# Graph layers: 24,000 of 100,000 edges counted once into small matrices and multiplied, the others gathered as before

## The chip, the cores and the metric

One Trainium2 chip, one of its cores. The metric is the device time of one launch in microseconds (us). TensorE (PE) multiplies, VectorE (DVE) and ScalarE (ACT) work elementwise, GpSimd (POOL) issues the indirect DMAs (gathers and scatters), SyncE (SP) issues the plain ones. SBUF has 128 partitions; PSUM has eight banks of 128 x 512 f32.

## The reference

3125 nodes with 256 features, 100,000 edges (src, dst, relation 0 to 3), all f32. Cut to what matters:

```
h   = x @ W0                                       # first layer
x   = layernorm(x + segment_sum(h[src] * norm, dst))
cnt[dst, type] += 1;  inv = 1 / max(cnt[dst, type], 1)
for l in 0..3:                                     # four relational layers
    h   = einsum('ni,rio->rno', X, weights[l])     # 4 tables of 3125 x 256
    agg = segment_sum(h[type, src] * inv, dst)
    out = agg + X @ root[l] + bias[l]
    X   = elu(layernorm(out) * gamma + beta) + X
result = layernorm(x + X)
```

The sources are drawn evenly over the nodes; the targets are the square of a uniform number, so low nodes have many edges.

## The kernel before, in words

Nodes are cut in 25 **windows** (NW) of 128 by target. The kernel has a set-up and five passes over the edges (q = 0 for the first layer, 1 to 4 for the relational ones).

**Set-up.** Edges lie as 125 x 800 in SBUF. DVE counts the edges of each window (L783), works out how many tiles of 128 edges each window needs, orders the windows by size, and gives every edge its rank in its window: a loop over the 25 windows (L839 to L851) of a hit row (L834), a running sum (L845) and a predicated copy (L851). Then the edges are sorted into tiles (L893 on, PE L554 to L567): in 50 iterations of 16 edge columns, 10 columns are placed by one-hot matmuls (L563, tile_hot against a 806-column row in two halves) and 6 by scatters of POOL (L408). L566 counts edges per node and relation. DVE decodes the placed edges (L926 to L943). There are NT = 806 tiles, a bound that is known before the run.

**A pass** does for each tile t, in this order of dependence:
- POOL gathers 128 rows of 256 f32 from the table of h in DRAM (L425) into one of RING = 20 slots. Gather n waits until the product of tile n - 20 is done (L424).
- A 128 x 128 **edge matrix** (one-hot of target times weight) is written into a ring of BODY = 32: in pass 0 by ACT (L681 Square, L690 Relu), later by DVE (L951), HALF = 16 tiles ahead.
- PE multiplies edge matrix and gathered rows into one of NPS = 6 banks (L533).
- DVE adds the bank to the accumulator of the tile's window (L976). The window's number comes from a list that is loaded into registers eight at a time (L961). In pass 0 DVE also finds each edge's weight first (L968).

Each engine's order is written out by hand. A window is complete after tile done_at[j] = (j + 1) * NT // 25. Its **window work** follows at fixed tiles after that: DVE norm and activation (L1031 to L1066, at +0 to +11), ACT Sqrt, Exp and copies (L607, L618, L622 to L637, each waiting its turn in one queue), PE transpose (L482, +15), four products of 512 columns with the next layer's weights (L490, +19 to +22) and the root product (L500, L503, +26, +27). SP writes the window's new rows of h to DRAM (L365). Pass q + 1 starts its gathers when the last window's rows are written (L421).

PE's matmul in f32 appears in the trace as two records, so a product of one tile is "x2".

Of the kernel before, what the change touches and what calls it, by code (L numbers as in the profile page):

```python
# [19 lines left out]
def build_program(nc, x, src, dst, etype, w0, weights, roots, biases, gammas, betas, out,  # L20
                  h0_table, h_tables, inv_dram, x1_dram, placed_dram):
    f32, f16, i32 = mybir.dt.float32, mybir.dt.float16, mybir.dt.int32
    ALU = mybir.AluOpType
# [14 lines left out]
    NT = (E + NW * (P - 1)) // P  # L38
    HALF = 16
    BODY = 2 * HALF  # L40
    RING = HALF + 4
    WINS = 8


    done_at = [(j + 1) * NT // NW for j in range(NW)]
    NPS = 6
# [5 lines left out]
    HB = NT // 2  # L52
    assert HB * 2 == NT and HB <= 512 and EC % SU == 0
# [6 lines left out]
    LOW = 1 << LOWBITS  # L60

    ctx = ExitStack()
    with ctx:
# [3 lines left out]
        def sem(name):  # L67
# [7 lines left out]
        iota16 = sb("iota16", [P, NT], f16)  # L75
        zeros16 = sb("zeros16", [P, 512], f16)
# [12 lines left out]
        X1 = arena[:, 0:NW * D]  # L89
# [3 lines left out]
        msg = sb("msg", [P, HALF, D])  # L93
        idx = sb("idx", [P, 2 * SS], i32)
        emat = sb("emat", [P, BODY, P])
        found = sb("found", [P, 2, R, P], f16)
# [16 lines left out]
        square = hout[:, 1:3, :].rearrange("p a b -> p (a b)")  # L113
        assert HALF * P == 2 * R * D

        slots = [msg[:, k, :] for k in range(HALF)] + [hout[:, CW - 1, k * D:(k + 1) * D]
                                                       for k in range(RING - HALF)]
# [21 lines left out]
        rw_hot = tmp(SU * R * NW // 2, f16).rearrange("p (b s n) -> p b s n", b=2, s=SB)  # L139
        assert at[0] <= 12800  # L140

        tile_hot = (arena[0:EP, 0:SR * NT // 2].bitcast(f16)
                    .rearrange("p (s n) -> p s n", s=SR))
        assert SR * NT // 2 <= 5 * EC + EC // 2 + EC
# [6 lines left out]
        assert 4 * batch + 2 * SR * P <= 2 * BODY * P  # L151
        flat = emat[:, :, :].rearrange("p a b -> p (a b)")

        placed = flat[:, 0:2 * NT].rearrange("p (t v) -> p t v", v=2)
        assert 3 * NT <= BODY * P
        win_ge = flat[0:NW, 2 * NT:3 * NT]
        a_i = msg[:, 0:4, :].rearrange("p a b -> p (a b)")[:, 0:NT].bitcast(i32)
        b_i = msg[:, 4:8, :].rearrange("p a b -> p (a b)")[:, 0:NT].bitcast(i32)
        c_i = msg[:, 8:12, :].rearrange("p a b -> p (a b)")[:, 0:NT].bitcast(i32)
        tot = sb("tot", [P, NW])  # L160
        n_tiles_i = sb("n_tiles_i", [P, NW], i32)
        n_tiles = sb("n_tiles", [P, NW])
# [5 lines left out]
        pick = sb("pick", [NW, NW])  # L168
        order_col = sb("order_col", [NW, 1])
        first_col = sb("first_col", [NW, 1])  # L170
        t_start = sb("t_start", [P, NW])
# [3 lines left out]
        run0 = sb("run0", [P, NW])  # L175
# [7 lines left out]
        banks = [ctx.enter_context(nc.psum_tensor(f"bank{i}", [P, 512], f32)) for i in range(8)]  # L183
# [73 lines left out]
        s_decoded = sem("s_decoded")  # L257
        s_outn = sem("s_outn")
# [14 lines left out]
        def window_at(eng, j):  # L273

            return nc.values_load_multi_w_load_instructions(
                order_i[0:1, bass.ds(j, 1)], engines=[eng], min_val=0, max_val=NW - 1,
                skip_runtime_bounds_check_because="a window's number is below NW")[1][0]

# [6 lines left out]
        def _(sp):  # L285
# [44 lines left out]
            with sp.Fori(0, NC) as c:  # L330
                for j in range(CW):
# [9 lines left out]
                         .to_broadcast([P, R * NPAD])).then_inc(s_inv_b, 16)  # L341
            for q in range(L + 1):
# [36 lines left out]
        def _(pool):  # L379
# [3 lines left out]
            pool.iota(iota16[:, :], [[1, NT]], base=0, channel_multiplier=0,  # L383
                      allow_small_or_imprecise_dtypes=True)
            pool.memset(zeros16[:, :], 0.0)
# [12 lines left out]
            pool.memset(flat[:, 0:2 * NT], 0.0).then_inc(s_clear, 1)  # L398
# [15 lines left out]
            def gather(q, table, rows):  # L414
# [7 lines left out]
                for t in range(NT):  # L422
                    n = q * NT + t
                    pool.wait_ge(s_mm, MM0 + n + 1 - RING)  # L424
# [10 lines left out]
        def _(pe):  # L435
# [21 lines left out]
            def edge_sums():  # L457

                pe.wait_ge(s_tot, 1)
                pe.matmul(misc_ps[0:EP, 0:NW], before[:, :], tot[0:EP, :], start=True, stop=True  # L460
                          ).then_inc(s_mm, MM0)
                pe.matmul(misc_ps[:, 64:64 + NW], ones[0:EP, :], tot[0:EP, :],
                          start=True, stop=True).then_inc(s_base, 1)

            def first_products():
# [4 lines left out]
                for w in range(NW):  # L470
                    if w == NW // 2:
# [34 lines left out]
            def window_work(q):  # L506


                first, work = (15 if q else 11), {}
                for j in range(NW):  # L510
                    n, at0 = q * NW + j, done_at[j] + first
                    work[at0] = lambda n=n: window_transposed(q, n)
                    for i in range(2 * KT):
                        h, k = divmod(i, KT)
                        work[at0 + 4 + i] = lambda n=n, h=h, k=k: window_product(q, n, h, k)
                    for k in range(KT):
                        work[at0 + 7 + 2 * KT + k] = lambda n=n, k=k: window_root(q, n, k)
                return work

            def aggregate(q):  # L520
# [3 lines left out]
                work = window_work(q) if q < L else {}  # L524
                for t in range(NT):
                    n = q * NT + t
                    if t in work:
                        work[t]()
# [6 lines left out]
                for at in sorted(work):  # L535
                    if at >= NT:
                        work[at]()
# [4 lines left out]
            for half in range(2):  # L542
                mm = pe.matmul(banks[6 + half][0:1, 0:HB], order_col[:, :],
                               win_ge[:, half * HB:(half + 1) * HB], start=True, stop=True)
            mm.then_inc(s_wmm, 1)
# [29 lines left out]

            for q in range(L + 1):
# [3 lines left out]
        def _(act):  # L580
# [6 lines left out]
            act.sem_inc(s_hev, BUF)  # L587

# [54 lines left out]

            def serve_messages(q, last=False):
# [525 lines left out]
```

## Time and profile before

| | us |
|---|---|
| three runs, median (lowest, highest) | 5897.99 (5896.36, 5899.21) |
| the profiled execution | 5900.55 |
| its span, first to last instruction | 5898.8 |
| set-up until the first gather | 688 |
| pass 0, then passes 1 to 4 | about 1030 to 1060, then 1020 to 1037 each |

Busy over the span: PE 78%, DVE 71%, POOL 72%, ACT 25%. The mean granted clock of TensorE is 0.739 of 2.4 GHz; it has two levels, 1.2 and 2.4 GHz. The page gives busy time, a chain of what ended last, and the costliest groups; the views by stage and in order of time are needed to see what paces a stage.

### The profile page before, as it was taken

How to read it: one execution, taken by the hardware profiler on the slowest of the kernel's cores; microseconds unless marked ns; L12 is line 12 of the kernel's file. 1: busy time of each engine (PE TensorE's matmuls, PEld its weight loads, DVE VectorE, ACT ScalarE, POOL GpSimd, SP SyncE). 2: the span in 40 equal slices, each digit the busy share in tenths (PEclk: the TensorE clock that was granted, in tenths of full speed). 3: DMA queues.
4: the chain of work that ended last, by engine and by line, in shares of the span. 5: the costliest groups of instructions: out<-in, count | busy, mean ns of one | idle time of the engine just before them, and what ended most of it. 6: DMA issues, size and time to landing. Idle time of an engine off the chain costs nothing.

```text
span 5898.8 us, 61567 instructions
## 1 busy us (share of the span) xinstructions
PE 4580.2 (78%) x12629; PEld 2337.2 (40%) x12629; DVE 4189.9 (71%) x10916; ACT 1463.4 (25%) x3865; POOL 4261.8 (72%) x4345
## 2 busy tenths in 40 slices
PE   2777588888877777787787788777787878888886
PEld 1444344444434444443444444333444433333333
DVE  8888788888876666665666666566666656666665
ACT  1666655555531111111111111111111110000000
POOL 0888677777757777776777777677777767777776
PEclk7999867777677777877777777777877765565655
DMA  1000344443443444344344444444443443333334
GB/s 48 1 1 1 107 120 121 120 122 114 121 127 116 116 120 119 116 120 112 116 116 119 119 116 119 112 116 116 119 120 115 120 103 105 105 105 105 105 105 107
DMA packets 280560, 616.88 MB, mean 105 GB/s; under 512 B 77007, under 2 KB 150561, under 8 KB 280152
## 3 DMA queue, kind: packets, MB, share of 16 engines
q0 software_dynamic: 203040, 529.13, 32.7%
q1 hardware_dynamic: 77240, 84.68, 4.5%
q8 instruction: 94, 1.54, 0.1%
q14 instruction: 186, 1.52, 0.1%
HBM read 549.83 MB, written 63.36 MB: 104 GB/s over the span
## 4 chain that ended last, share of the span: by engine, by line
PE 50%; DVE 18%; issue 18%; DMA 4%; POOL 3%; ACT 3%; DVEq 3%; SPq 0%; POOLq 0%; ACTq 0%
PE bank L533 41%; DVE arena L976 9%; PE bank L490 6%; DVE emat L951 5%; POOL placed_dram L408 3%; DMA placed_dram<-leaving,idx 3%; DVE found L968 2%; DVEq L961 1%; PE bank L500 1%; ACT hout L681 1%; ACT emat L690 1%; PE bank L503 1%; PE bank L482 1%; DVEq L976 1%; DVE wstats L1031 0%
## 5 line engine op out<-in xcount | busy, mean ns | idle before, releaser
L533 PE MATMUL bank<-msg,emat 128*128 128x256 f32 x6452 | 2901.4, 557 | 813.5 <-DVE emat L951 382.8
L425 POOL DMA_INDIRECT msg<-h_table,g_rel x2580 | 2449.2, 949 | 875.5 <-issue 477.9
L976 DVE TENSOR_TENSOR arena<-arena,bank 128x256 f32 x4030 | 1686.0, 418 | 1242.2 <-PE bank L533 1206.2
L533 PEld LDWEIGHTS bank<-msg,emat 128*128 128x128 f32 x6452 | 1389.5, 256 | 2355.3 <-DVE emat L951 1483.2
L951 DVE TENSOR_SCALAR emat<-iota,node,weight 128x128 f32<-128x128 f32 x3224 | 1183.7, 369 | 194.8 <-DVE arena L976 65.6
L533 PE MATMUL bank<-hout,emat 128*128 128x256 f32 x1608 | 719.6, 554 | 188.5 <-DVE emat L951 90.7
L425 POOL DMA_INDIRECT msg<-h_table,g_src x646 | 616.6, 955 | 227.5 <-issue 134.2
L425 POOL DMA_INDIRECT hout<-h_table,g_rel x644 | 610.9, 949 | 221.2 <-issue 116.7
L968 DVE SCALAR_TENSOR_TENSOR found<-iota,key,arena 128x512 f16<-128x512 f32 x806 | 605.9, 752 | 130.4 <-issue 20.8
L408 POOL DMA_INDIRECT placed_dram<-leaving,idx x300 | 428.6, 1429 | 232.1 <-issue 213.5
L533 PEld LDWEIGHTS bank<-hout,emat 128*128 128x128 f32 x1608 | 349.6, 257 | 564.6 <-DVE emat L951 356.9
L563 PE MATMUL bank<-arena,emat 125*128 125x403 f16 x2000 | 385.3, 336 | 188.6 <-ACT emat L719 109.9
L490 PE MATMUL bank<-w_sb,xt 128*128 128x512 f32 x800 | 456.5, 658 | 22.3 <-ACT xt L626 22.3
L607 ACT ACTIVATE wsd<-wmv,eps_col 128x1 f32<-128x1 f32 x125 | 36.8, 295 | 1276.1 <-DVE wmv L1036 1140.0
L690 ACT ACTIVATE emat<-hout,ones 128x128 f32<-128x128 f32 x806 | 285.3, 395 | 229.8 <-PE bank L533 226.6
L719 ACT ACTIVATE emat<-emat,arena 125x128 f16<-125x128 f16 x1000 | 303.0, 387 | 10.1 <-DVE emat L879 1.6
L563 PEld LDWEIGHTS bank<-arena,emat 125*128 125x128 f16 x2000 | 164.8, 97 | 314.4 <-issue 123.4
L632 ACT COPY hout<-bank 128x512 f32<-128x512 f32 x200 | 116.1, 581 | 645.1 <-PE bank L490 645.1
L681 ACT ACTIVATE hout<-iota,neg_node 128x128 f32<-128x128 f32 x806 | 241.0, 387 | 4.2 <-DMA h_table<-hout 2.6
L490 PEld LDWEIGHTS bank<-w_sb,xt 128*128 128x128 f32 x800 | 171.2, 216 | 66.6 <-ACT xt L626 28.9
L900 DVE TENSOR_SCALAR arena<-iota,arena 125x806 f16<-125x806 f16 x500 | 195.9, 426 | 0.0
L425 POOL DMA_INDIRECT hout<-h_table,g_src x160 | 151.8, 949 | 50.3 <-issue 32.6
(152 smaller groups left out, 2112.4 us busy)
## 6 DMA issues: line engine op xcount, KB each, us to landing
h_table<-hout SPq DMA_DIRECT2D x100, 512.0 KB, 3.3
msg<-h_table,g_rel POOLq DMA_INDIRECT x2580, 2.8
msg<-h_table,g_src POOLq DMA_INDIRECT x646, 2.8
hout<-h_table,g_rel POOLq DMA_INDIRECT x644, 2.8
arena<-inv_dram SPq DMA_DIRECT2D x1, 6400.0 KB, 20.1
placed_dram<-leaving,idx POOLq DMA_INDIRECT x300
w_sb<-in_L_gnn_weights_dram SPq DMA_DIRECT2D x8, 512.0 KB, 5.3
h_table<-hout SPq DMA_DIRECT2D x25, 128.0 KB, 1.7
```

The lines of the kernel that those rows point to most:

```text
L408: pool.indirect_dma_start(out=placed_dram[:, :], out_offset=bass.IndirectOffsetOnAxis(ap=idx[0:EP, n:n + 1], axis=0), in_=leaving[:, n, :] ...
L425: pool.indirect_dma_start(out=slots[n % RING], out_offset=None, in_=table[:, :], in_offset=bass.IndirectOffsetOnAxis(ap=rows[:, t:t + 1], ...
L490: mm = pe.matmul(win_ps[h][:, :], xt[:, 0, k * P:(k + 1) * P], w_sb[:, k, 2 * h:2 * h + 2, :].rearrange("p r o -> p (r o)"), start=(k == 0 ...
L533: pe.matmul(agg_ps[n % NPS][:, 0:D], emat[:, n % BODY, :], slots[n % RING], start=True, stop=True).then_inc(s_mm, 1)
L563: pe.matmul(ps[half][:, 0:HB], slot[:, n, :], tile_hot[:, n, half * HB:(half + 1) * HB], start=False, stop=False)
L681: a = act.activation(square[:, i * P:(i + 1) * P], iota[:, 0:P], ACT.Square, bias=neg_node[:, t:t + 1])
L690: act.activation(emat[:, t % BODY, :], square[:, i * P:(i + 1) * P], ACT.Relu, bias=ones[:, 0:1], scale=-1.0).then_inc(s_em, 1)
L719: a = act.activation(slot[:, n, :], lane_hot[:, b, m, :], ACT.Copy, scale=val[:, bass.ds(i * SU + k, 1)])
L900: dve.tensor_scalar(tile_hot[:, n, :], iota16[0:EP, :], pos_hi[:, bass.ds(t + m, 1)], None, ALU.is_equal).then_inc(s_hot, 1)
L951: dve.tensor_scalar(emat[:, n % BODY, :], iota[:, 0:P], node[:, t:t + 1], weight[:, t:t + 1], ALU.is_equal, ALU.mult).then_inc(s_em, 1)
L968: dve.scalar_tensor_tensor(found[:, t % 2, :, :], key_v, key[:, t:t + 1], inv_v[:, :, bass.ds(w, 1), :].rearrange("p r w d -> p r (w d)"), ...
L976: dve.tensor_tensor(a, a, agg_ps[n % NPS][:, 0:D], ALU.add).then_inc(s_acc, 1)
```

## The change

24,000 edges (at most), those whose source lies in one of the six **chunks** (128 source nodes) with most edges, become **dense**:

- Set-up: DVE counts edges per source chunk too, ranks the 25 chunks, takes the top K = 6, and moves the window number of such an edge to one of 50 extra bins (25 windows x H = 2 halves of KH = 3 chunks). Counting and ranking loops run over NB = 75 bins where they ran over 25. By the formulas there are NT = 618 tiles to gather, DT = 238 dense tiles, NTA = 856 in the sort.
- **build_counts** (once, between sort and pass 0): per dense tile DVE writes two one-hot rows (384 source slots, 512 relation-and-target keys, f16); PE multiplies them into a set of three PSUM banks: three matmuls of 512 columns, and before each tile three that end a set and three of 512 columns that begin one (at a real set or at a bank nobody reads, NOWHERE). The bank addresses come from registers. ACT copies each finished set to int16 and stores it in DRAM (**flush_counts**, 50 sets).
- Every pass: SP loads the six chunks' rows of h into SBUF (**load_cache**, 6 x 512 KB, in pass 0 6 x 128 KB). For each window ACT converts six 128 x 512 blocks of counts to f32 (**convert**, three buffers) and loads the next window's counts (2 x 393 KB); PE does 24 products count block x cached rows of 256 columns (**dense_product**) between the tiles, accumulated in two banks; DVE adds them to the window, scaled by 1/count, in four operations (one in pass 0; **dense_added**, at done_at[j] - 2).
- Smaller rings: HALF 16 -> 8, BODY 32 -> 16, NPS 6 -> 4; RING stays 20. `found` has one buffer.
- Each pass of SP now waits for the last rows written before it loads the cache and then the weights.

```diff
-    NT = (E + NW * (P - 1)) // P
-    HALF = 16
+    KH, H = 3, 2
+    K = KH * H
+    NDE = E * K // NW
+    NT = (E - NDE + NW * (P - 1)) // P
+    DT = (NDE + NW * H * (P - 1)) // P
+    DT += (NT + DT) % 2
+    NTA = NT + DT
+    NB = NW * (1 + H)
+    HALF = 8
     BODY = 2 * HALF
+    MSGS = 16
+    RING = MSGS + 4
-    NPS = 6
+    NPS = 4
...
+        def dense_tile(j, i):
+            d = done_at[j - 1] if j else 0
+            return d + 4 + i * 16 // (K * R) if j else 14 + i * 7 // (K * R)
...
             for q in range(L + 1):
                 if q > 0:
+                    sp.wait_ge(s_hs, (q * NW + ONE0) * 16)
+                    load_cache(q)
                     sp.wait_ge(s_hm, q * NW)
...
+            def dense_product(q, j, i):
+                n, (c, r) = q * NW + j, divmod(i, R)
+                m = n * K + c
+                if i == 0:
+                    pe.wait_ge(s_hc, (q + 1) * (16 * K))
+                    if n:
+                        pe.wait_ge(s_dense, n)
+                if r == 0:
+                    pe.wait_ge(s_conv, m + 1)
...
+                mm = pe.matmul(to, blocks[m % AF][:, r * P:(r + 1) * P], rows,
+                               start=(c == 0 and first), stop=(c == K - 1 and last))
+                if r == R - 1:
+                    mm.then_inc(s_used, 1)
...
+            def build_counts():
+                begin_set(NOWHERE)
+                for c in range(KH):
+                    begin_set(c * R * P)
+                for t in range(DT):
+                    k = t % FEW
+                    if k == 0:
...      (after, sets, edges: three loads of 4, 8 and 8 values into registers, FEW = 4)
+                    if t:
+                        pe.wait_ge(s_free, after[k])
+                        for c in range(KH):
+                            mm = end_set(bank_at(shut, step, c))
+                            if c == KH - 1:
+                                mm.then_inc(s_built, 1)
+                            begin_set(bank_at(opened, step, c))
+                    pe.wait_ge(s_oh, t + 1)
+                    for c in range(KH):
+                        pe.matmul(cols(psum, at + c * R * P if c else at, R * P),
+                                  src_hot[t % OH][:, c * P:(c + 1) * P], key_hot[t % OH],
+                                  start=False, stop=False)
...
+            def convert(n, c):
+                m, (h, k) = n * K + c, divmod(c, KH)
+                if k == 0:
+                    act.wait_ge(s_counts[h], (n + 1) * 16)
+                if m >= AF:
+                    act.wait_ge(s_used, m - AF + 1)
+                act.copy(blocks[m % AF], counts[:, h, k * R * P:(k + 1) * R * P]
+                         ).then_inc(s_conv, 1)
...
             def serve_messages(q, last=False):
+                for c in range(K):
+                    convert(q * NW, c)
                 for j in range(NW):
                     n = q * NW + j
                     v = window_at(mybir.EngineType.Activation, j)
                     window_sd(n)
+                    if j + 1 < NW:
+                        for c in range(4):
+                            convert(n + 1, c)
                     window_exp(n - NW)
+                    if j + 1 < NW:
+                        for c in range(4, K):
+                            convert(n + 1, c)
...
+            totals(s_hi, NW, tot_s)
...
+            totals(d_hi, NB, tot)
...
-            with dve.Fori(0, NW // CW) as i:
+            with dve.Fori(0, NB // CW) as i:
...
+            for t in range(DT):
+                if t >= OH:
+                    dve.wait_ge(s_built, t - OH + 1)
+                dve.tensor_scalar(src_hot[t % OH], iota16[:, 0:KH * P], d_slot[:, t:t + 1], None,
+                                  ALU.is_equal)
+                dve.tensor_scalar(key_hot[t % OH], iota16[:, 0:R * P], d_key[:, t:t + 1], None,
+                                  ALU.is_equal).then_inc(s_oh, 1)
...
+            def dense_added(q, j):
...
+                    for r in range(R):
+                        if r:
+                            dve.wait_ge(s_dstep, (n - NW) * (R - 1) + r)
+                        s = dve.scalar_tensor_tensor(
+                            a, dense_ps[r // 2][:, r % 2 * D:(r % 2 + 1) * D],
+                            cols(inv, v + r * NW, 1), a, ALU.mult, ALU.add)
```

## Rows read from the trace of the kernel before

**Rows 1.** The page, part 4: share of the chain that ended last, by engine.

```profile
PE 50%; DVE 18%; issue 18%; DMA 4%; POOL 3%; ACT 3%; DVEq 3%; SPq 0%; POOLq 0%; ACTq 0%
```

**Rows 2.** Stages: span, busy us per engine (instructions), granted clock, DMA share, GB/s.

```profile
17.00:147.00 130.00, 35.11 (x163) 27.61 (x163) 126.32 (x176) 17.52 (x54) 0.72 (x1) 0.68 0.09 29
147.00:663.00 516.00, 403.17 (x2801) 232.85 (x2802) 458.11 (x802) 335.72 (x1199) 425.51 (x298) 0.99 0.07 1
708.00:1737.00 1029.00, 843.89 (x1994) 424.78 (x1993) 905.33 (x2539) 564.07 (x1712) 753.21 (x790) 0.71 0.41 118
1750.00:2786.00 1036.00, 805.54 (x2012) 424.34 (x2012) 666.15 (x1812) 139.94 (x225) 764.30 (x806) 0.76 0.42 120
4858.00:5878.00 1020.00, 857.15 (x1612) 381.37 (x1612) 678.46 (x1907) 85.72 (x120) 765.76 (x806) 0.59 0.38 104
```

**Rows 3.** Order of time: start, us, engine, line; first gathers of pass 2.

```profile
2786.01 0.94 POOL L425 DMA_INDIRECT msg<-h_table,g_rel  x1 [26.48 <-DMA h_table<-hout]
2787.25 0.95 POOL L425 DMA_INDIRECT msg<-h_table,g_rel  x1 [0.30 <-issue]
```

**Rows 4.** Order of time, pass 0: DVE, one tile to the next.

```profile
716.23 0.75 DVE L968 SCALAR_TENSOR_TENSOR found<-iota,key,arena 128x512 f16<-128x512 f32 x1
...
717.47 0.75 DVE L968 SCALAR_TENSOR_TENSOR found<-iota,key,arena 128x512 f16<-128x512 f32 x1
```

**Rows 5.** Order of time, set-up: PE, f32 products of 256 columns at clock 1.00.

```profile
35.70 1.03 PE L453 MATMUL bank<-w_sb,xt 128*128 128x256 f32 x4
...
36.56 0.38 PE L444 MATMUL bank<-ident,X 128*128 128x128 f32 x2
...
36.78 1.03 PE L453 MATMUL bank<-w_sb,xt 128*128 128x256 f32 x4
```

**Rows 6.** Stages as Rows 2, inside pass 1: tiles alone, then with window work.

```profile
2563.00:2578.00 15.00, 14.03 (x25) 6.01 (x24) 10.17 (x29) 0.82 (x2) 11.35 (x12) 0.50 0.36 105
2578.00:2593.00 15.00, 11.01 (x36) 6.14 (x34) 9.24 (x23) 1.54 (x3) 11.35 (x13) 0.95 0.47 139
```

**Rows 7.** Order of time, end of pass 4: one tile's product at the low clock.

```profile
5869.69 1.19 PE L533 MATMUL bank<-msg,emat 128*128 128x256 f32 x2 [0.58 <-issue]
```

**Rows 8.** Order of time, set-up: DVE, counting one window to the next.

```profile
28.52 1.04 DVE L783 TENSOR_SCALAR_CACHE_REDUCE arena<-arena,iota 125x800 f16<-125x800 f16 x1
...
29.48 1.04 DVE L783 TENSOR_SCALAR_CACHE_REDUCE arena<-arena,iota 125x800 f16<-125x800 f16 x1
```

**Rows 9.** Order of time, set-up: DVE, first running sum and the end of the loop.

```profile
64.69 1.88 DVE L845 TENSOR_TENSOR_SCAN arena<-arena,run 125x800 f32<-125x800 f32 x1 [0.35 <-DVE arena L834]
...
140.86 0.58 DVE L854 CAST arena<-arena 125x800 int32<-125x800 f32 x1
```

**Rows 10.** Groups of 0 to 200 us: operations like those the set-up gains.

```profile
L834 DVE TENSOR_SCALAR arena<-arena,iota 125x800 f16<-125x800 f16 x26 | 10.4, 401 | 0.0
...
L808 DVE TENSOR_TENSOR msg<-msg,n_tiles 128x625 f32<-128x625 f32 x1 | 0.8, 812 | 0.0
```

**Rows 11.** Order of time, sort: PE, four f16 matmuls of 403 columns and one of 100.

```profile
305.50 0.85 PE L563 MATMUL bank<-arena,emat 125*128 125x403 f16 x4
...
306.23 0.85 PE L563 MATMUL bank<-arena,emat 125*128 125x403 f16 x4
```

**Rows 12.** DVE's register loads, eight values each: ns min/median/max.

```profile
L961 DVEq TENSOR_LOAD <-win_i x505: 591/597/1755, 707.8 to 5867.8; - x169
```

**Rows 13.** Groups of ACT, 1800 to 2750 us, shapes kept apart.

```profile
L607 ACT ACT_TABLE_LOAD x23 | 29.5, 1283 | 0.4
...
L632 ACT COPY hout<-bank 128x512 f32<-128x512 f32 x47 | 27.5, 585 | 198.4 <-PE bank L490 198.4
```

**Rows 14.** The page, part 6: KB each, us to landing.

```profile
h_table<-hout SPq DMA_DIRECT2D x100, 512.0 KB, 3.3
...
arena<-inv_dram SPq DMA_DIRECT2D x1, 6400.0 KB, 20.1
```

**Rows 15.** Order of time: DVE between decode and pass 0.

```profile
686.26 5.39 DVE L946 MEMSET arena<- 128x6400 f32 x1 [4.35 <-issue]
...
708.81 0.75 DVE L968 SCALAR_TENSOR_TENSOR found<-iota,key,arena 128x512 f16<-128x512 f32 x1 [17.16 <-issue]
```

More of the change, by code:

```diff
@@ L181, in build_program @@
         deg_s = sb("deg_s", [P, NW])
-        banks = [ctx.enter_context(nc.psum_tensor(f"bank{i}", [P, 512], f32)) for i in range(8)]
+        psum = ctx.enter_context(nc.psum_tensor("psum", [P, 8 * 512], f32))
+        banks = [psum[:, i * 512:(i + 1) * 512] for i in range(8)]
+        assert 2 * AW <= 6 * 512
+        dense_ps = banks[4:6]
         agg_ps = banks[0:NPS]
@@ L257, in build_program @@
         s_decoded = sem("s_decoded")
+        s_oh = sem("s_oh")
+        s_built = sem("s_built")
+        s_free = sem("s_free")
+        s_stored = [sem(f"s_stored{h}") for h in range(H)]
+        s_counts = [sem(f"s_counts{h}") for h in range(H)]
+        s_conv = sem("s_conv")
+        s_used = sem("s_used")
+        s_hc = sem("s_hc")
+        s_dstep = sem("s_dstep")
+        s_dense = sem("s_dense")
         s_outn = sem("s_outn")
@@ L277, in window_at, with put, run @@
                 skip_runtime_bounds_check_because="a window's number is below NW")[1][0]
+        def dense_tile(j, i):
+            d = done_at[j - 1] if j else 0
+            return d + 4 + i * 16 // (K * R) if j else 14 + i * 7 // (K * R)
+        def put(work, t, step):
+            work.setdefault(t, []).append(step)
+        def run(work, t):
+            for step in work.get(t, ()):
+                step()
         def apart(eng):
@@ L534, in aggregate @@
                               start=True, stop=True).then_inc(s_mm, 1)
-                for at in sorted(work):
-                    if at >= NT:
-                        work[at]()
+                for late in sorted(work):
+                    if late >= NT:
+                        run(work, late)
             first_products()
@@ L574, in _, with begin_set, end_set, bank_at @@
             pe.wait_ge(s_decoded, 1)
+            def begin_set(at):
+                return pe.matmul(cols(psum, at, R * P), zeros16[:, 0:P], zeros16,
+                                 start=True, stop=False)
+            def end_set(at):
+                return pe.matmul(cols(psum, at, 1), zeros16[:, 0:P], zeros16[:, 0:1],
+                                 start=False, stop=True)
+            def bank_at(first, step, c):
+                return nc.s_assert_within(first + step * c if c else first, 0, NOWHERE,
+                                          skip_runtime_bounds_check_because="its set or NOWHERE")
@@ L685, in serve_first @@
                     for i, t in enumerate(tiles):
-                        if t in work:
-                            work[t]()
+                        run(work, t)
                         if t >= BODY:
@@ new lines, in _ @@
+            a_d, b_d, c_d, e_d = (v[:, NT:NTA] for v in (a_i, b_i, c_i, e_i))
+            done(dve.scalar_tensor_tensor(d_key[:, :], a_d, float(P), b_d, ALU.mult, ALU.add))
+            done(dve.tensor_scalar(e_d, c_d, P - 1, None, ALU.bitwise_and))
+            done(dve.tensor_copy(d_slot[:, :], e_d))
+            done(dve.tensor_scalar(c_d, c_d, 7, None, ALU.arith_shift_right))
+            chunk, part = e_d.bitcast(f32), a_d.bitcast(f32)
+            done(dve.tensor_copy(chunk, c_d))
+            for i in range(K):
+                if i % KH:
+                    done(dve.tensor_scalar(part, chunk, top[:, i:i + 1], float(i % KH * P),
+                                           ALU.is_equal, ALU.mult))
+                    done(dve.tensor_tensor(d_slot[:, :], d_slot[:, :], part, ALU.add))
@@ L1119, in window_steps @@
                 for j in range(NW):
+                    steps[done_at[j] - 2] = lambda j=j: dense_added(q, j)
                     for i in after:
```

418 lines of the change are left out of this document (324 added, 94 removed).

## The prediction

> **What bounds the kernel now.** I read the page first. Its chain gives PE 50% [rows 1], which would say that TensorE paces the passes. The stages say otherwise. In pass 1 POOL issues 806 gathers in 1036 us and is busy 764 us of them [rows 2]; in order of time one gather follows the other at 1.25 us, 0.95 busy and 0.30 of issue [rows 3]. 806 x 1.25 = 1007 us; the other 28 us of a pass are the gap in which POOL waits for the last window's rows to be written, 26.5 us at the start of pass 2 [rows 3]. So **passes 1 to 4 go at POOL's rate**, and PE, which follows POOL through a ring of 20 slots, is in the chain only because it stands last in each hand-over. Pass 0 goes at DVE's: one tile to the next is 1.24 us [rows 4], DVE busy 905 of 1029 us [rows 2]; POOL's 1.25 is just beside it. The set-up is DVE (126 of 130 us), then the sort with DVE at 458 and PE at 403 of 516 us [rows 2].
>
> TensorE's clock: tiles alone, at 1.25 us each, run at 0.50 though PE is recorded busy 14.0 of 15 us, because at 1.2 GHz each product is stretched; when window products come in between, the clock is 0.95 [rows 6].
>
> **The change, part by part.**
>
> *Fewer gathers (passes 1 to 4).* 806 - 618 = 188 gathers fewer, x 1.25 = 235 us a pass, x 4 = **-940**. The 28 us gap stays: it is the last window's chain, which the change leaves. That holds if nobody is slower than POOL, whose window is now 24.7 x 1.25 = 30.9 us.
>
> PE per window at 2.4 GHz: one 256-column f32 product is 0.43 us in a stream, half of the 0.86 between the start of two products and the transposes behind them [rows 5]. 24.7 tiles are 10.6 us, 24 dense products 10.3, the window work (four of 512 columns, two roots, bias, transposes) some 4.9: **25.8 of 30.9 us**. At 1.2 GHz it would be 51. A single product is 0.67 us at the high clock by its own length and 1.19 at the low one [rows 7]. PE is busy four fifths of the time at the high clock, about what the second stretch of [rows 6] shows, and only tiles +20 to +27 (with window products in them) and +0 to +3 are thin, so I expect a mean near 0.95 and some 2 us a window lost.
>
> One stall is new: ACT's queue. The root's copy waits for PE at done_at + 27, which was five tiles before the next window's end and is now two tiles behind it. Behind it stand a table load, 1.28 us [rows 13], the Sqrt, and then convert 0, which takes about 0.59 us as the 128 x 512 copy does [rows 13]. So convert 0 is done near tile +5 where PE asks for it at +4: 1.6 us a window. DVE waits about a microsecond for the Sqrt at +4. PE's window becomes 25.8 + 2 + 1.6 = 29.4 us. This fits below 30.9, and the ring of 20 slots (25 us of gathers) evens it out. DVE: 24.7 tiles of 0.8 us, window work near 3.5 and four dense additions of 0.5 are 25 us; below POOL. NPS = 4 holds 5 us of gathers against the 2.3 us that DVE is away. The counts' loads, 2 x 393 KB a window, add 25 GB/s to a DMA that is 42% busy [rows 2], while gathers fall by nothing per us; hidden. load_cache is 3 MB, about half of the 6.4 MB that took 20.1 us [rows 14], and PE asks for it at tile 14 (17 us plus the first gather's 5): a lag of up to 10 us in PE, which the ring takes. For all these I add 10 us a pass: **+50** (0 to 60 a pass; the upper end is the first rival).
>
> *Pass 0.* DVE saves 188 x 1.24 = 233 us and gains 25 dense additions of 0.45 and a wait, 0.65 each: 16. **-217**. ACT has 24.7 x 0.6 + 6 converts + window work, 22 of 31 us.
>
> *Set-up loops.* Ranking takes 76.2 us for 25 windows [rows 9], 3.05 each; 50 more bins: +152.5. Counting is 0.96 a bin [rows 8]; 25 chunks and 75 bins for 25: 75 x 0.97 = +72.5. Both are on DVE, with nothing beside it that ends later: **+225**. The small steps (six times compare and add over 800 f16, 0.4 and 0.5 to 1.0; a second running sum 1.9; about fourteen 625-element operations of 0.81 [rows 10]; two trips to PE; nine list operations after the ranking) sum to **+36** (25 to 55).
>
> *Sort.* 100 half-iterations of 5.16 us [rows 2]. tile_hot and matmuls grow by 6%: five tiles of 0.04 on PE's tail and DVE's share: +0.1 each, **+10** (0 to 25).
>
> *Build.* Serial: pass 0 waits for it on PE, DVE and ACT. Per dense tile PE streams 3 x 512 columns and begins 3 x 512; 1712 columns take 0.735 us [rows 11], so 3072 take 1.32, with three one-column ends about **1.45 us, the lower end**. No row shows an f16 matmul whose bank comes from a register, or PE's own register work. The upper end takes every one of the nine matmuls alone, 0.38 us, with no overlap, and the loads serial: three of 0.6 us [rows 12] per four tiles, 0.45: **3.9 us**. I take 2.0: streaming plus the loads plus 0.1, since PE's sequencer has much to do here and the loads are the one part with a row. 238 x 2.0 = 476 us. DVE's two one-hots, about 0.5, and ACT's three copies of 0.59 per set of some five tiles are below that; the two set buffers hide the stores (3.3 us for 512 KB [rows 14]). DVE's memset ends at 691.7 and the first tile's work now begins at 708.8 [rows 15]; after: 691.7 + 476 + 5 (last set) + 8 (stores, first counts, eight edge matrices) = 1181. **+472**. The load of the inverse counts, for which DVE waited 17 us [rows 15], hides in it.
>
> Sum: 5900.6 - 940 - 217 + 50 + 225 + 36 + 10 + 472 = 5537; the profiled execution stands 2.6 above the median of the runs: **5535 us**.
>
> **A rule weighed.** The stretch of tiles alone stays at 0.50 for 15 us with PE recorded busy nearly throughout [rows 6]. The Trainium skill (TensorE: Matmul & The Clock Gate, "Part 1: The HAM clock gate") says that "the default state is throttled, and activity releases the throttle". By the rule the denser stream of the changed passes goes at 2.4 GHz and the sum is as above; by the row, if recorded busyness is not what counts and 1.2 GHz stayed, PE's window would be 51 us and the time 5535 + 125 x 20 = 8040. The sort, with PE busy 403 of 516 us, ran at 0.99 [rows 2]; that bears the rule out.
>
> **Rivals.**
> - *PE paces the passes* (dense products with their waits on blocks, clock drops in the thin tiles). For it: the margin is 1.5 us of 30.9, in-order waits on ACT. Against: backlog lets PE stream, and stream means high clock. At 32.5 us a window: 5535 - 50 + 125 x 1.6 = 5685; at 34: 5870.
> - *The same, slower than before*: from 34.3 us a window (5900) on it decides; at 36 us (mean clock about 0.75 with the same work) 5535 - 50 + 125 x 5.1 = 6120. Against it: pass 1 had 0.76 with 806 products and the window work [rows 2], and would now have half as many again.
> - *Build is dear*: 3.0 us a tile (each address waits for its register) is 5773; at 3.9, 5987, slower than before; it decides from 3.5.
> - *All smooth*: build 1.5, no friction: 5535 - 119 - 50 = 5366.
> - *It doesn't do what it says*: no; 618 gathers a pass are written out.
>
> **How the numbers follow.** Forecast 0.50 (own range 5430 to 5640), smooth 0.14, PE paces but faster 0.13, build dear but faster 0.08, PE slower 0.07, build slower 0.04, clock stays low 0.02, 0.02 near the old time. The range leaves out the slower cases and the fastest tail: 5340 to 5830. Within 0.2%, about what a measurement of this kernel tells from no change, 0.02; slower 0.13; faster 0.85.
>
> **What would show it.** Gathers at 1.25 us with "issue" ahead of them through passes 1 to 4, passes near 810 us, granted clock above 0.9: right. POOL waiting for PE's product before most gathers, passes over 850: the first rival. The end of the sort near 935 us shows the set-up's +270; the span between the last decode step and the first product of pass 0, divided by 238, gives the build's price per tile. Convert 0 as what PE waits for at done_at + 4 shows the ACT stall.

## The result and the profile after

The changed kernel takes **5587.5 us**, median of 4 runs (5585.06 to 5591.9), against 5898.6 us of the kernel before on the same chip (5896.36 to 5900.36). The ratio is 0.9474, 95% interval 0.9457 to 0.949. The profiled execution took 5589.8 us, its span is 5587.8. The forecast was 5535 with a range of 5340 to 5830: right in sign and inside the range, 52 us too low. By the stages below one term, pass 0, was 67 us short; the others came out some 15 us better between them.

The page of the kernel after, its fourth part: shares of the chain that ended last, by engine and by line. It answers to [rows 1]; PE's share rose, and the new products (L656) stand first in it.

```profile
PE 64%; DVE 15%; issue 12%; ACT 5%; DVEq 3%; DMA 1%; ACTq 0%; SPq 0%
```

The stages of the kernel after, columns as in [rows 2]: span; busy us and instructions of PE, PE's weight loads, DVE, ACT and POOL; granted clock, DMA share, GB/s. In order: ranking and small steps, from the end of counting to the sort's start; the sort; the build of the counts; pass 0; passes 1 to 4.

```profile
145.50:404.60 259.10, 20.86 (x89) 14.45 (x88) 256.47 (x288) 8.69 (x27) 2.78 (x3) 0.53 0.00 0
404.60:930.00 525.40, 437.91 (x2802) 223.03 (x2803) 465.30 (x804) 336.05 (x1199) 433.12 (x298) 0.99 0.07 1
957.00:1441.00 484.00, 386.80 (x2134) 178.04 (x2135) 138.66 (x475) 76.60 (x147) 19.16 (x20) 0.92 0.15 57
1449.50:2350.50 901.00, 762.41 (x2836) 551.15 (x2836) 717.28 (x2011) 545.31 (x1555) 581.61 (x599) 0.92 0.44 128
2350.50:3160.20 809.70, 719.27 (x2836) 555.95 (x2836) 557.65 (x1536) 223.81 (x374) 588.67 (x619) 0.93 0.52 151
3160.20:3972.50 812.30, 724.42 (x2836) 558.41 (x2836) 558.05 (x1536) 225.07 (x375) 588.01 (x618) 0.92 0.51 147
3972.50:4781.50 809.00, 719.40 (x2836) 555.15 (x2836) 556.81 (x1536) 225.03 (x375) 588.18 (x618) 0.93 0.51 147
4781.50:5587.80 806.30, 656.40 (x2436) 480.93 (x2436) 576.00 (x1652) 174.31 (x273) 588.25 (x618) 0.88 0.47 133
```

The reader can make the sum from this. Before, pass 1 began at 1749.8 us and passes 1 to 4 took 4149.0 us; they take 3237.3 now (-911.7). Pass 0 took 1041.0 us from its first tile [rows 15] to pass 1, and takes 901 (-140). The first tile's work stands at 1449.5, not 708.8 (+740.7). Together -311.0, which is 5587.8 less 5898.8.

The first gathers of pass 2 in order of time, the answer to [rows 3]: start, us, engine, line, tiles, idle before and its releaser.

```profile
3160.20 0.94 POOL L532 DMA_INDIRECT hout<-h_table,g_rel  x1 [33.08 <-DMA h_table<-hout]
3161.45 0.95 POOL L532 DMA_INDIRECT hout<-h_table,g_rel  x1 [0.30 <-issue]
```

The cadence is the old 1.25 us. The gap ahead of this pass is 33.1 us where it was 26.5: it is the last window's chain. PE's last product of a tile now ends 14.5 us after the last gather's start (10.5 before), and then come the window's four dense additions, 0.6 us each. Ahead of passes 1 to 4 it is 39.6, 33.1, 34.9 and 32.8 us, before 37.6, 26.5, 25.3 and 26.4.

What PE, ACT and POOL waited for in pass 0 (1450 to 2340 us): us in total, times, longest. In the first row 469 us are the build, ahead of the pass.

```profile
POOL msg L532 <- PE psum L678: 591.7, 153, 469.1
ACT emat L855 <- PE psum L656: 236.5, 108, 4.1
...
PE psum L621 <- ACT hout L833: 83.8, 23, 4.8
DVE arena L1332 <- PE psum L678: 69.5, 47, 7.3
```

L855 is ACT's convert, which waits until PE has used up a block (L656); L621 is PE's root product, which waits for ACT's copy of half of the window's products (L833). One such wait, on ACT in order of time:

```profile
1715.60 0.62 ACT L855 CAST emat<-counts 128x512 f32<-128x512 int16 x1
1719.50 0.62 ACT L855 CAST emat<-counts 128x512 f32<-128x512 int16 x1 [3.28 <-PE psum L656]
1724.23 0.62 ACT L855 CAST emat<-counts 128x512 f32<-128x512 int16 x1 [4.12 <-PE psum L656]
...
1725.26 1.86 ACT L947 ACTIVATE emat<-hout,ones 128x128 f32<-128x128 f32 x6 [0.40 <-PE psum L678]
1727.03 0.56 ACT L833 COPY hout<-psum 128x512 f32<-128x512 f32 x1
```

and on PE right behind it:

```profile
1727.64 0.70 PE L621 MATMUL psum<-root_sb,xt 128*128 128x256 f32 x2 [2.15 <-ACT hout L833]
```

ACT stood idle for 7.4 us in two converts whose blocks PE was not done with; then six edge matrices had to go first, and only then the copy, for which PE was by now waiting. An engine that is busy 545 of 901 us seems to hold up the pass by its order; the experiments test that.

### The profile page after: what moved, and what is told of

Read it like the earlier page. It is cut to its first block, busy times and chain, and to the rows that moved or that the text cites. A ratio compares the mean times of both kernels' runs of the same rounds, so it can differ in the third digit from the quotient of the medians.

```text
span 5587.8 us, 75729 instructions
## 1 busy us (share of the span) xinstructions
PE 4454.3 (80%) x18899; PEld 3136.3 (56%) x18899; DVE 3972.8 (71%) x10123; ACT 1842.1 (33%) x4389; POOL 3399.9 (61%) x3405
## 4 chain that ended last, share of the span: by engine, by line
PE 64%; DVE 15%; issue 12%; ACT 5%; DVEq 3%; DMA 1%; ACTq 0%; SPq 0%
PE psum L656 23%; PE psum L678 21%; PE psum L611 6%; PE psum L709 6%; DVE arena L1332 4%; PE psum L723 3%; DVE arena L1474 3%; PE psum L765 3%; DVE arena L1219 2%; DVE arena L1232 1%; ACT hout L939 1%; DVE emat L1307 1%; ACT emat L855 1%; ACT emat L947 1%; PE psum L621 1%
## 5 line engine op out<-in xcount | busy, mean ns | idle before, releaser
L532 POOL DMA_INDIRECT msg<-h_table,g_rel x1978 | 1882.4, 952 | 671.1 <-issue 403.9
L1332 DVE TENSOR_TENSOR arena<-arena,psum 128x256 f32 x3090 | 1291.9, 418 | 793.9 <-PE psum L678 766.7
L678 PE MATMUL psum<-msg,emat 128*128 128x256 f32 x4948 | 1564.6, 411 | 222.9 <-DVE arena L1332 85.3
L656 PE MATMUL psum<-arena,emat 128*128 128x256 f32 x4800 | 1408.2, 407 | 118.7 <-ACT emat L855 118.4
L678 PEld LDWEIGHTS psum<-msg,emat 128*128 128x128 f32 x4948 | 962.4, 204 | 617.2 <-DVE emat L1307 255.7
L656 PEld LDWEIGHTS psum<-arena,emat 128*128 128x128 f32 x4800 | 973.4, 206 | 323.4 <-issue 185.8
L855 ACT CAST emat<-counts 128x512 f32<-128x512 int16 x750 | 442.4, 615 | 959.7 <-PE psum L656 957.9
L514 POOL DMA_INDIRECT placed_rows<-leaving,idx x300 | 435.9, 1453 | 487.0 <-issue 458.3
L709 PE MATMUL psum<-arena,emat 125*128 125x428 f16 x2000 | 427.0, 347 | 320.6 <-DVE arena L1232 320.6
L611 PE MATMUL psum<-w_sb,xt 128*128 128x512 f32 x800 | 414.1, 602 | 7.0 <-ACT xt L827 7.0
L833 ACT COPY hout<-psum 128x512 f32<-128x512 f32 x200 | 116.2, 581 | 640.9 <-PE psum L611 640.8
```

The lines of the kernel that those rows point to most:

```text
L514: pool.indirect_dma_start(out=placed_dram[:, :], out_offset=bass.IndirectOffsetOnAxis(ap=idx[0:EP, n:n + 1], axis=0), in_=leaving[:, n, :] ...
L532: pool.indirect_dma_start(out=slots[n % RING], out_offset=None, in_=table[:, :], in_offset=bass.IndirectOffsetOnAxis(ap=rows[:, t:t + 1], ...
L611: mm = pe.matmul(win_ps[h][:, :], xt[:, 0, k * P:(k + 1) * P], w_sb[:, k, 2 * h:2 * h + 2, :].rearrange("p r o -> p (r o)"), start=(k == 0 ...
L656: mm = pe.matmul(to, blocks[m % AF][:, r * P:(r + 1) * P], rows, start=(c == 0 and first), stop=(c == K - 1 and last))
L678: pe.matmul(agg_ps[n % NPS][:, 0:D], emat[:, n % BODY, :], slots[n % RING], start=True, stop=True).then_inc(s_mm, 1)
L709: pe.matmul(ps[half][:, 0:HB], slot[:, n, :], tile_hot[:, n, half * HB:(half + 1) * HB], start=False, stop=False)
```

## The experiments

The chips of these runs were three others than the first, and slower for both kernels: before took 6626 to 6627 us on each of them. The changed kernel was therefore run on one of them as well, and all stages below are compared with that run. The traces of these chips hold only a fifth to a quarter of the records of the gathers' landings (for the ring's first slot 637 in the changed kernel's, where the first chip's trace has 2480). So part of a wait is put down there to "issue" or "remote", and where a total of idle time is given below, it is the engine's idle time just before the operation, whatever ended it.

**The changed kernel again.**

> The changed kernel itself, run again beside the experiments, because the kernel before now takes 6626 us and not 5899 (its first runs were on another chip). If the slowdown is one of gathers (a pass of 618 gathers 955 us and not 810, of which kernels with pass 0 unchanged show 985 to 996 us for pass 0), this kernel takes 5588 + 4 x 145 + 90 = about 6265 us, ratio to before 0.945 to 0.947. With its own time the parts that the experiments took off can be read as differences.

Measured: 6267.96 us median (6256.16 to 6276.6), ratio 0.9459 (0.9442 to 0.9476), the same as on the first chip. Its stages: build, pass 0, pass 1.

```profile
957.00:1462.50 505.50, 390.20 (x2141) 179.08 (x2141) 139.53 (x479) 81.22 (x160) 19.12 (x20) 0.91 0.15 56
1462.50:2455.40 992.90, 798.41 (x2836) 576.10 (x2836) 724.85 (x2011) 548.39 (x1555) 577.60 (x599) 0.88 0.40 116
2455.40:3411.50 956.10, 777.95 (x2836) 575.18 (x2836) 540.61 (x1536) 222.41 (x374) 587.68 (x619) 0.86 0.44 128
```

The set-up up to the build is where it was (first one-hot at 957.1 us, 956.7 on the first chip); what has gathers in it is slower. For pass 0 there are five kernels that leave it as it was: 993, 988, 996, 985 and 990 us. They lie within 11 us; what differs by more is the edit's. Both waits of the first chip are there: PE is idle for 83.7 us before the root product (83.8 there), ACT for 314.8 us before the converts (236.5 there).

**PE's root product later.**

```diff
-put(work, at0 + 7 + 2 * KT + k, lambda: window_root(q, n, k))
+put(work, at0 + (7 if q else 11) + 2 * KT + k, lambda: window_root(q, n, k))
-put(work, at0 + 25, lambda: window_root_out(j, number[j]))
+put(work, at0 + 27, lambda: window_root_out(j, number[j]))
```

> In pass 0 PE's root product stands four tiles later (at done_at + 26 and + 27 as in passes 1 to 4, before: + 22 and + 23), and ACT's copy of the root two places later. Nothing is left out. Pass 0 took 901 us where 834 were forecast. Theory A (ACT's queue is late): in pass 0 PE waits at the root product for ACT's copy of half of the window's products, 83.8 us over 23 windows, because ACT, which should stand 16 tiles ahead, is held by converts that wait for a block to come free; four tiles more give it 5 us. Pass 0 shortens by 50 to 80 us, to about 835, and the time is about 5525. Rival B (PE itself, 762 of 901 us busy, is what pass 0 cannot go below with the small waits between its products): the wait moves from the root product to another product, pass 0 shortens by less than 15 us, time 5575 to 5590.

Measured: 6237.87 us (6211.89 to 6247.03), ratio 0.942 (0.9403 to 0.9437). The same kernel once more:

> The same kernel as before with only PE's root product four tiles later, looked at again where gathers go at 1.25 us. Theory A: pass 0 from 901 to about 835 to 850 us, time about 5530. Rival B (PE itself paces pass 0): 885 or more. If DMA-bound gathers were what held pass 0 at 961 on the other chip, both go below 961 here.

Measured: 6235.65 us (2 runs), ratio 0.9413 (0.9394 to 0.9432). Gathers did not go at 1.25 us throughout here either, so this is a repetition and not the test that was meant. Pass 0 of the two:

```profile
1459.80:2421.00 961.20, 782.13 (x2836) 539.85 (x2836) 723.43 (x2011) 539.22 (x1555) 582.52 (x599) 0.92 0.41 120
```

```profile
1462.70:2415.30 952.60, 779.42 (x2836) 542.76 (x2836) 722.28 (x2011) 539.19 (x1555) 581.74 (x599) 0.92 0.42 121
```

That is 32 and 40 us less than 993: more than rival B allowed, less than theory A wanted. The waits of pass 0 in the first of the two say why:

```profile
ACT emat L856 <- PE psum L657: 232.1, 76, 9.5
PE psum L603 <- ACT hout L815: 43.1, 12, 7.2
PE psum L621 <- ACT hout L834: 11.0, 12, 1.4
```

PE's idle time before the root product fell from 83.7 us to 12.7, but the converts (L856) wait as long as ever, 316.8 us in all for 314.8, and ACT is as late as before for PE's transposes (L603, 51.4 us in all for 56.8). Half of what was gained is lost again before the tiles' own products, where PE is now idle for 80 us and was for 29. Moving the one that waits treats one place at a time.

**A quarter of the dense products in pass 0.**

```diff
+if r < R - 1:
+    return
-to, first, rows = dense_ps[0][:, 0:D], r == 0, hcache0[c]
+to, first, rows = dense_ps[0][:, 0:D], True, hcache0[c]
```

> In pass 0 only 6 of each window's 24 dense products are made (one for each chunk, at the place of the chunk's last, so that blocks come free at the same tiles); the sums of the other 18 are left out. Theory A (ACT's queue delays the copy for which PE's root product waits): PE saves 18 x 0.43 = 7.7 us a window, but waits for the same copy; pass 0 shortens by less than 40 us. Rival B (PE's own work paces pass 0): up to 7.7 x 25 = 190 us of which DVE (717 us busy, 0.8 for a tile and its waits) lets through about 80 to 110: pass 0 at about 800.

Measured: 6231.62 us (2 runs), ratio 0.9406 (0.9387 to 0.9425). Pass 0:

```profile
1461.90:2422.30 960.40, 651.65 (x1936) 396.78 (x1935) 720.46 (x2011) 547.55 (x1554) 579.07 (x599) 0.84 0.40 120
```

18 products a window are gone, 147 us of PE's recorded time (798.4 less 651.7), and pass 0 is shorter by 32.5 us, no more than by moving one product. PE only stood idle for longer, before the root product 105.9 us and not 83.7. PE's own work is not what paced it. Rival B is out.

**ACT's converts later, nothing else.**

```diff
-if c < AF:
-    t = dense_tile(j, 0)
-elif j:
-    t = done_at[j - 1] + BODY + (4, 5, 9)[c - AF]
+if j:
+    t = done_at[j - 1] + (6, 9, 11, BODY + 6, BODY + 9, BODY + 12)[c]
+elif c < AF:
+    t = dense_tile(j, 0)
```

> Only the converts of pass 0 are placed later, as above; root, transposes and window products stand where the change put them, the build is unchanged. Theory A: the half-out copies come in time for PE's root product at done_at + 22, and pass 0 falls from 985 to 996 us to 930 to 950, as much as by moving the root product or more. Rival C (the wait is for ACT's work in itself, 22 us of 36 per window with bursts of eight squares, not for the blocks): less than 15 us.

Measured: 6198.89 us (2 runs), ratio 0.9352 (0.9333 to 0.9371). Pass 0, and the waits in it:

```profile
1460.80:2384.80 924.00, 779.20 (x2836) 548.52 (x2836) 720.19 (x2011) 549.49 (x1555) 583.82 (x599) 0.91 0.43 125
```

```profile
ACT emat L947 <- PE psum L678: 224.1, 162, 4.9
ACT emat L855 <- PE psum L656: 11.9, 4, 9.5
PE psum L621 <- ACT hout L833: 1.4, 2, 0.8
```

69 us less, more than expected, with ACT's work unchanged (549.5 us busy, 548.4 in the changed kernel). The converts' wait is gone (314.8 to 11.9 us in all) and with it the root product's (83.7 to 1.6). ACT's idle time has not vanished: it is now at L947, where ACT has made 16 edge matrices ahead and waits for PE to use one. That wait holds nobody up, since nothing that PE needs soon is queued behind it. Rival C is out, and theory A is shown on these chips, with its place: the wait of a convert for a block, with the copy behind it. On the first chip the same waits stand in the trace, but no edit was run.

**The combined versions.** One puts pass 0's root product four tiles later, its transposes one and its window products two, and takes the assertions out of the build (below); the other adds the later converts.

```diff
-put(work, at0, lambda n=n: window_transposed(q, n))
+put(work, at0 + (0 if q else 1), lambda n=n: window_transposed(q, n))
-put(work, at0 + 4 + i, lambda: window_product(q, n, h, k))
+put(work, at0 + (4 if q else 6) + i, lambda: window_product(q, n, h, k))
```

> The root product of pass 0 four tiles later, its transposes one and its window products two tiles later, and a bitwise and in place of each of PE's bounds assertions in the build. Nothing is left out. By the first runs, on a chip where gathers took longer (a pass 955 us, which is also a floor under pass 0), the and saves 54 us of the build, and the later root product 30 us of pass 0, down to about that chip's floor. Where a pass takes 810 us again, theory A (ACT's queue was late for PE's root product) expects pass 0 at 901 less 55 to 75 us and the whole at 5588 - 54 - 65 = about 5470 us, ratio to before 0.927. Rival B (PE's own work paces pass 0): pass 0 no lower than 885, time 5515 to 5535.

Measured: **6132.33 us** (6125.61 to 6145.91), ratio 0.9264 (0.9248 to 0.9279): the ratio that was forecast for a chip on which a pass takes 810 us (0.927), met on one where passes take 933 to 963. Both kernels are slower there, so this doesn't test the 5470 us that went with it.

> As the combined version (masks in the build, root, transposes and window products of pass 0 later), and ACT's converts of pass 0 so placed that none waits for a block that PE frees within the next 16 tiles: chunks 0 to 2 two, five and seven tiles after the window's begin (all at four before), chunks 3 to 5 at 6, 9 and 12 (4, 5 and 9 before) plus the 16. Nothing is left out. Theory A (ACT's lead over PE, 16 tiles at most, is used up by converts that wait): pass 0 another 15 to 40 us shorter than the 920 of the combined version; if the chip's gathers are its floor (618 at 1.25 plus this chip's stalls, some 910 to 930), nothing more than 10. Time 6100 to 6130, ratio 0.922 to 0.926. Rival (order of ACT's converts is of no account): the same as the combined version within 5 us.

Measured: 6150.24 us (6136.89 to 6156.13), ratio 0.9278 (0.9262 to 0.9294); the two intervals overlap. Pass 0 of the first and of the second:

```profile
1406.40:2326.00 919.60, 770.70 (x2836) 539.38 (x2836) 718.91 (x2011) 539.24 (x1555) 582.62 (x599) 0.93 0.43 125
```

```profile
1407.70:2323.00 915.30, 774.19 (x2836) 528.40 (x2836) 718.70 (x2011) 545.99 (x1555) 582.67 (x599) 0.94 0.43 126
```

All three roads end at 915 to 924 us. In the first combined version the converts still wait, 270 us in all: moving all three kinds of products behind ACT's lateness does as much as removing it. That the roads end alike agrees with a floor of these chips' gathers, but no run took the gathers away, so the floor is argued and not shown. Against the changed kernel the first combined version is 0.9264 / 0.9459 = 0.979 (each against before, whose times on the two chips are 6625.8 and 6626.7 us; 0.977 to 0.982 by the two intervals), the lowest time measured here. On the first chip it was not run; by that ratio it would be near 5470 us, an estimate.

**A mask for the build's assertions.**

```diff
 _, after = values_load(after_i[0:1, part], min_val=1, max_val=ND,
+                       skip_runtime_bounds_check_because="a set's number")
-pe.wait_ge(s_free, after[k])
+pe.wait_ge(s_free, after[k] & 127)
```

> In the build of the counts the four bounds assertions on PE per group of four tiles (1.16 us by the profile) are gone; each wait takes its value through a bitwise and with 127 instead, one register operation. Nothing is left out. Theory: PE's sequencer paces the build (register loads 1.5 us, assertions 1.16 and about 1.2 us of addressing and issue for each tile, 7.45 of 7.95 us per four tiles): the build falls from 486 us by 60 groups x (1.16 less 4 x 0.15) = 34 us or a little more, up to 70 if the and is free; time about 5550. Rival (the streaming of six 512-column matmuls and three ends, 1.37 us a tile, paces it, and loads are hidden behind it): under 10 us.

Measured: 6213.9 us (6182.15 to 6222.74), ratio 0.9367 (0.9336 to 0.9399). The build:

```profile
956.00:1406.00 450.00, 358.76 (x2141) 181.01 (x2141) 139.20 (x478) 81.24 (x161) 18.94 (x20) 0.97 0.17 64
```

From 505.5 to 450: 55 us, by an edit of register operations alone. With the denser stream the granted clock rose from 0.91 to 0.97, and PE's recorded busy time fell by 31 us for the same products.

**Half as wide products in the build.**

```diff
-pe.matmul(cols(psum, at + c * R * P if c else at, R * P),
-          src_hot[t % OH][:, c * P:(c + 1) * P], key_hot[t % OH],
+pe.matmul(cols(psum, at + c * R * P if c else at, 2 * P),
+          src_hot[t % OH][:, c * P:(c + 1) * P], key_hot[t % OH][:, 0:2 * P],
```

> In the build each dense tile's three products go over 256 columns and not 512 (the counts of two of the four relations are left out); the number of instructions, register loads and assertions is the same. Streaming falls from 1.37 to about 1.04 us a tile. If PE's sequencer paces the build (7.45 us of issue per four tiles): build shorter by less than 30 of 486 us. Rival (streaming and the gap at the register loads add up): 238 x 0.33 = 78 us shorter.

Measured: 6261.54 us (2 runs), ratio 0.9451 (0.9426 to 0.9476). The build, and two of its tiles' products in order of time:

```profile
956.00:1457.60 501.60, 348.52 (x2141) 205.16 (x2141) 138.78 (x476) 81.15 (x160) 18.76 (x20) 0.85 0.15 57
```

```profile
1201.56 0.49 PE L765 MATMUL psum<-emat 128*128 128x256 f16 x3
...
1203.31 0.85 PE L765 MATMUL psum<-emat 128*128 128x256 f16 x3
```

4 us less where streaming would have given 78. The clock, granted at 0.91 in this stage, is at 0.85 now, and in the second of the two rows it is at 0.50, the level of 1.2 GHz (0.96 in the first). But PE is also idle 153 of 502 us, so width was not what paced it. The two runs together show that PE's sequencer does. From one group of four tiles to the next, on the sequencer, take the medians: in the changed kernel 8.0 us, of which 2.84 are loads and assertions and the rest 1.29 a tile; with half the width 2.83 and 1.28; without assertions 1.63 and 1.36.

**Fewer products in passes 1 to 4, and more.**

```diff
+if q and 0 < c < K - 1 and r < R - 1:
+    return
```

> In passes 1 to 4 only 12 of each window's 24 dense products are made (all of chunks 0 and 5, the last of the others); the sums of the other 12 are left out. PE saves 12 x 0.43 us x 25 = 129 us of work a pass. My theory (POOL's 618 gathers at 1.25 us set passes 1 to 4): the passes stay at 810, within 10 us each, but for the last window's gap, up to 7 us shorter; time 5555 to 5588. Rival (PE paces them, 719 of 810 us busy, and POOL follows): 60 to 129 us less a pass, time under 5350.

Measured: 6229.66 us (2 runs), ratio 0.9404 (0.9385 to 0.9423). Pass 1:

```profile
2446.60:3391.90 945.30, 683.38 (x2236) 463.44 (x2236) 531.06 (x1536) 220.72 (x374) 588.12 (x619) 0.83 0.44 129
```

The four passes are shorter by 11, 3, 1 and 9 us than in the changed kernel, for 95 us less of PE's recorded time in a pass; kernels that leave pass 1 alone differ by more (943 to 966 us). PE's work does not pace them on these chips.

```diff
 mm = pe.matmul(to, blocks[m % AF][:, r * P:(r + 1) * P], rows, ...)
+if q and c in (1, 2, 4):
+    mm = pe.matmul(to, blocks[m % AF][:, r * P:(r + 1) * P], rows,
+                   start=False, stop=False)
```

> In passes 1 to 4 12 of each window's 24 dense products (those of chunks 1, 2 and 4) are made twice, so that these counts enter double; PE gets 129 us more work a pass: 719 + 129 = 848 of 810. It shows how much room PE had. With PE's waits as small as they are, passes of 860 to 900 us, time 5790 to 5950. If PE had hidden room (records longer than its real work, a lower clock that rises with more work): 820 to 845 us, time under 5730.

Measured: 6494.44 us (2 runs), ratio 0.9804 (0.9784 to 0.9823). Pass 1:

```profile
2450.70:3477.00 1026.30, 872.55 (x3436) 680.03 (x3436) 564.09 (x1536) 223.51 (x374) 586.71 (x618) 0.90 0.41 119
```

Half as many products again cost 70, 79, 75 and 16 us in the four passes, in the middle of the forecast for a pass of 810 (50 to 90). So PE stands close beside the bound: of 129 us added, little over 50 fitted in. What more chunks in the dense part would bring, with fewer gathers beside more products, was not run.

## Why the prediction came out as it did

- **Passes 1 to 4** (-940, and 10 us of friction a pass): -900 forecast, -912 measured. 809.7, 812.3, 809.0 and 806.3 us against 810. POOL's cadence is the bound, as argued: 618 x 1.25 and a gap of 33 us are 806. The friction is there in another form, 2 to 10 us more of gap at each pass's start. The reason is shown by the trace of the first chip: in pass 1 POOL starts 604 of 617 gathers at most 1.35 us after the one before, and the longest step is 1.51 us. The run with fewer products adds that PE's work isn't the pace, but on chips whose gathers do not keep that cadence.
- **Ranking, counting, small steps** (+225 and +36): the sort begins at 404.6 and not at 145.8 us, +259 against +261. From the end of counting to the sort DVE is busy 256.5 of 259.1 us.
- **Sort** (+10): it takes 525.4 us, some 8 to 9 more.
- **Build and hand-over** (+472): the one-hots begin at 956.7, the build ends near 1441.5, 485 us or 2.04 a tile, for which 2.0 was taken between 1.45 and 3.9. The size was right and the reason half right: it was written as streaming plus loads, with the sequencer as an addition. The runs show the sequencer as the pace: about 1.3 us of issue a tile, 1.5 us of loads and 1.16 us of assertions per four tiles, 4 x 1.3 + 2.66 = 7.9 us or 1.97 a tile. The assertions had not been seen in the code; they were 55 us in the run without them. So the 2.0 is in part luck: it was 1.45 for streaming, 0.45 for loads and 0.1, and came out as 1.3 for issue, 0.38 for loads and 0.29 for assertions, two errors that cancel. First tile's work: +741 against +743.
- **Pass 0** (-217 and 10 of friction, so 834 us): measured 901. This is the term that was mis-sized, by 67 us. It was sized by DVE's load and gave ACT "22 of 31 us" a window as if ACT could do its work in any order. The prediction did look for an in-order stall on ACT, but in passes 1 to 4, at convert 0. In pass 0 a window took 36 us and not 33: ACT waited for blocks (236.5 us in all) with the copy behind them for which PE's root product waited (83.8 us). Moving the converts gave 69 us on the chips of the experiments, where pass 0 was 993 us; that this is as much as the 67 that were missing fits, but the edit was not run on the first chip, so how much of the 67 it would give back is not shown.
- **The rule weighed.** The clock in passes 1 to 4 is 0.93, 0.92, 0.93 and 0.88, as the denser stream was expected to bring (a mean near 0.95); pass 1 had 0.76 before [rows 2]. The runs agree from both sides, in pass 1: 0.83 with 12 products a window, 0.86 with 24, 0.90 with 36. This is what the Trainium skill says (TensorE: Matmul & The Clock Gate, "Part 1: The HAM clock gate"): activity releases the throttle.
- **The rivals.** PE as the pace of passes 1 to 4 did not come, though it is near: the run with more products puts its cost at some 75 us for 129 us of work. The dear build did not come. "All smooth" missed by the build, 2.04 us a tile and not 1.5 (some 128 us), and by pass 0.

## What to carry to other kernels

An engine that is busy six tenths of the time can pace a stage by its order alone: look in the waits for an instruction that waits for something not yet due, and for what stands behind it in the same queue. Moving the early one later is one edit for all its victims: placing the converts by when their blocks come free gave 69 us. Moving one victim, the root product, gave 32 to 40; it took all three kinds of products to reach 73. And where a matmul's address comes from registers, count the sequencer's instructions per matmul, bounds assertions included, before its columns.

## What the runs showed of the hardware

- On the three chips of the experiments gathers do not keep their 1.25 us. In pass 1 of the changed kernel 86 of 617 start over 2 us after the one before, on the first chip none; the trace shows most of them waiting for PE to free a slot of the ring. In order of time, POOL in pass 1 of the changed kernel there:

```profile
2911.18 0.94 POOL L532 DMA_INDIRECT msg<-h_table,g_rel  x1 [0.30 <-issue]
2913.40 0.94 POOL L532 DMA_INDIRECT msg<-h_table,g_rel  x1 [1.27 <-PE psum L678]
2915.55 0.94 POOL L532 DMA_INDIRECT msg<-h_table,g_rel  x1 [1.21 <-PE psum L678]
2916.80 0.97 POOL L532 DMA_INDIRECT msg<-h_table,g_rel  x1 [0.30 <-PE psum L678]
```

  A pass takes 956 us and not 810, before takes 6626 and not 5899 us, and the set-up up to the first one-hot is the same to 0.4 us in 957. PE with 95 us less to do hardly changes it. The build shows a piece of it: it takes 497.5 us and not 485.0, and all of the difference arises in its first eight tiles, while POOL issues the first 20 gathers of pass 0 (951 to 981 us). There nine of PE's register operations take some 0.7 us or more, where on the first chip none takes 0.2; after that the build goes at the first chip's rate. So beside gathers PE's sequencer is slow there, before any slot of the ring is in play. Between 2500 and 5500 us DVE has 265 gaps of over 2 us between the starts of two instructions, where it had 23 on the first chip. Whether the same makes PE late with the slots in the passes is open, and so is whether it lies in the chip; no run here separates a cause.
- A bounds assertion on PE's sequencer costs about 0.29 us a value with the operation ahead of it. Its two instructions alone are 152 and 18 ns. The register loads of the build, ns min/median/max, for four values and then for eight:

```profile
L743 PEldq FUSED_REGOPS  x238: 146/152/171, 950.5 to 1437.3; - x119
L743 PEldq SEQ_ASSERT  x238: 18/18/32, 950.7 to 1437.5; - x119
L743 PEldq TENSOR_LOAD <-hout x60: 330/334/706, 949.9 to 1436.4; - x60
...
L746 PEldq TENSOR_LOAD <-hout x60: 330/592/983, 951.7 to 1437.6; - x60
```

  Eight values cost PE what they cost DVE [rows 12].
